# Second attention: the first query weights of each group of heads loaded and split in the key projection's block

## The reference, cut to what matters

```python
q = (x @ Wq).reshape(B, S, 16, 128)      # Wq is 512 x 2048
k = (x @ Wk).reshape(B, S, 4, 128)       # Wk is 512 x 512
v = (x @ Wv).reshape(B, S, 4, 128)
q, k = rope(q), rope(k)
# the two halves of a head's 128 columns are two queries and two keys of 64 columns
a1 = softmax(mask(q1 @ k1.T / 8));  a2 = softmax(mask(q2 @ k2.T / 8))    # window of 128
d = relu(a1 - lam * a2);  d = d / (d.sum(-1) + 1e-6)
x = x + ((d @ v).reshape(B, S, 2048) @ Wo)
```

## Time and profile before

| | us |
|---|---|
| three runs, median (lowest to highest) | 2696.87 (2694.24 to 2699.04) |
| the profiled execution | 2698.5 |
| its span, first to last instruction | 2696.7 |

### The profile page before, as it was taken

One profiled execution on the slowest core, in us unless ns is written; L12 is line 12 of the kernel. 1 busy time (PEld: TensorE's weight loads), 2 busy tenths in 40 slices (PEclk: granted clock), 3 DMA queues, 4 the chain that ended last, 5 costly groups with the idle time before them and its releaser, 6 DMA issues. The chain is left out here.

```text
span 2696.7 us, 35818 instructions
## 1 busy us (share of the span) xinstructions
PE 2519.3 (93%) x12212; PEld 1693.6 (63%) x12212; DVE 1738.9 (64%) x3811; ACT 1112.5 (41%) x2809; POOL 1023.9 (38%) x757
## 2 busy tenths in 40 slices
PE   6899999999599999997879999969999889999998
PEld 3444444443288888886656777657777656557886
DVE  6677676665245555555538999839999823335886
ACT  1246555555232323231316777707776711111111
POOL 2348677775311111110006767615444410002442
PEclk9989999999899999999889999989999999999999
DMA  4721221203300000000212100010000088873101
GB/s 174 242 48 37 43 55 25 56 13 102 125 24 16 16 16 16 16 1 17 92 49 75 44 21 21 21 47 17 17 9 9 1 310 294 292 288 92 48 24 63
DMA packets 153639, 193.64 MB, mean 72 GB/s; under 512 B 52622, under 2 KB 98702, under 8 KB 153088
## 3 DMA queue, kind: packets, MB, share of 16 engines
q1 hardware_dynamic: 141952, 178.90, 20.8%
q0 software_dynamic: 11520, 12.64, 1.5%
HBM read 161.95 MB, written 54.53 MB: 80 GB/s over the span
## 5 line engine op out<-in xcount | busy, mean ns | idle before, releaser
L725 DVE TENSOR_REDUCE neg<-bank 128x1 fp32r<-128x1024 f32 x256 | 300.7, 1213 | 147.0 <-PE bank L629 146.6
L775 ACT ACTIVATE probs<-bank 128x512 f32<-128x512 f32 x512 | 289.4, 596 | 254.0 <-PE bank L639 237.4
L569 POOL TENSOR_TENSOR probs<-probs 128x1024 f32<-128x1024 f32 x128 | 301.9, 2382 | 172.3 <-PE bank L648 172.3
L1567 POOL TENSOR_SCALAR mix<-mix,sm 128x256 f32<-128x256 f32 (+1 forms) x256 | 232.5, 918 | 174.9 <-DVE sm L1464 174.4
L1507 ACT ACTIVATE ms<-ms,sm 128x256 f32<-128x256 f32 (+1 forms) x512 | 247.6, 486 | 94.4 <-DVE sm L1435 93.5
L639 PE MATMUL bank<-q_parts,k_parts 97*128 97x512 f32 x512 | 203.3, 444 | 1.7 <-ACT probs L775 0.7
L947 POOL TENSOR_TENSOR up_lo<-up_raw,up_hi 128x1024 fp32r<-128x1024 f32 x16 | 46.1, 2904 | 401.0 <-ACT up_hi L937 401.0
L1435 DVE CUSTOM_DVE_ANT_0 ms<-bank,misc 128x256 f32<-128x256 f32 (+1 forms) x512 | 184.8, 400 | 2.3
L629 PE MATMUL bank<-k_parts,q_parts 96*128 96x512 f32 x512 | 176.7, 434 | 6.9 <-DVE neg L725 5.0
L639 PEld LDWEIGHTS bank<-q_parts,k_parts 97*128 97x128 f32 x512 | 87.1, 189 | 146.1 <-ACT probs L775 124.2
L1017 DVE TENSOR_TENSOR hid<-bank,sg 128x512 f32<-128x512 f32 x64 | 44.3, 692 | 180.1 <-ACT sg L967 180.1
(11 more groups left out here) (225 smaller groups left out, 5900.9 us busy)
## 6 DMA issues: line engine op xcount, KB each, us to landing
ewg<-in_L_ffn_Wg_dram SPq DMA_DIRECT2D x32, 704.0 KB, 6.8
ewu<-in_L_ffn_Wu_dram SPq DMA_DIRECT2D x32, 704.0 KB, 8.1
ewd<-in_L_ffn_Wd_dram SPq DMA_DIRECT2D x32, 512.0 KB, 5.3
q_parts<-qk_dram SPq DMA_DIRECT2D x48, 256.0 KB, 4.4
up_raw<-in_L_ffn_W_dram SPq DMA_DIRECT2D x16, 512.0 KB, 4.1
ewd<-in_L_ffn_Wd_dram SPq DMA_DIRECT2D x32, 192.0 KB, 5.5
qk_dram<-qk_hi SPq DMA_DIRECT2D x20, 256.0 KB, 2.2
qk_dram<-qk_lo SPq DMA_DIRECT2D x20, 256.0 KB, 2.0
```

The source lines that it names most:

```text
L569: pool.tensor_tensor(probs[:, even, half, :], probs[:, even, half, :], probs[:, odd, half, :], ALU.add).then_inc(S["paired"], 1)
L725: dve.tensor_reduce(neg[:, U % HPT, q:q + 1], bank[:, 2 * (n % 2):2 * (n % 2) + 2, :], AX.XY, ALU.max, negate=True).then_inc(S["max"], 1)
L775: act.activation(probs[:, s % BUFS, j, :], bank[:, 4 + j % 2, :], ACT.Exp, scale=scale).then_inc(S["exps"], 1)
L1567: pool.tensor_scalar(mix[:, p % 2, h, 0:w], mix[:, p % 2, h, 0:w], sm[:, p % 3, 8 + h:9 + h], None, ALU.mult).then_inc(S["probs"], 1)
```

## The change

Pair 0 of each group leaves the heads block. The key block loads its query weights into `w` once VectorE has split the key weights (`klo`), ScalarE and GpSimd split them there into half 0 of `wh` and `wl`, and SyncE loads its output weights after that. The key weights are split into half 1 instead of half 0. In the second group the load of `v` is issued after the query load. In the heads block the four calls for pair 0 are gone; everything else there is as before.

```diff
--- before.py
+++ after.py
@@ -1222,7 +1222,9 @@
 
     ins, xh, xl, bank, ident = (env[k] for k in ("ins", "xh", "xl", "bank", "ident"))
     w, wh, wl, k_, v, rope, lam, tr = (t[k] for k in ("w", "wh", "wl", "k", "v", "rope", "lam", "tr"))
-    rounds = NC * g
+    wo = w[:, :, :].rearrange("p (h a) n -> p h (a n)", h=2)
+    rounds, PAIRS = NC * g, H1 // 4
+    head = 2 * g * PAIRS
 
     @block.sync
     def _(sp):
@@ -1231,9 +1233,20 @@
             sp.dma_start(lam[:, :], ins["L1_attn_lam"].partition_broadcast(P)).then_inc(S["lam"], 16)
             for half in ("woraw", "wraw"):
                 sp.wait_ge(S[half], CREDIT + 16 * NT // 2)
-        else:
+        sp.wait_ge(S["klo"], CREDIT + g + 2)
+        sp.dma_start(w[:, :, :], ins["L1_attn_Wq"].rearrange("(k p) n -> p k n", p=P)[:, :, head * P:(head + 2) * P]).then_inc(
+            S["wraw"], 16)
+        if g:
             sp.dma_start(v[:, :, :], env["v_dram"].rearrange("(n p) d -> p n d", p=P)).then_inc(S["kw"], 16)
+        sp.wait_ge(S["wlo"], CREDIT + g * PAIRS + 1)
+        sp.dma_start(wo, ins["L1_attn_Wo"].rearrange("(h p) n -> p h n", p=P)[:, head:head + 2, :]).then_inc(S["woraw"], 16)
+        if g:
             sp.wait_ge(S["kw"], CREDIT + 64)
+
+    @block.gpsimd
+    def _(pool):
+        pool.wait_ge(S["whi"], CREDIT + g * PAIRS + 1)
+        pool.tensor_tensor(wl[:, 0, :, :], w[:, :, :], wh[:, 0, :, :].bitcast(F32), ALU.subtract).then_inc(S["wlo"], 1)
 
     @block.tensor
     def _(pe):
@@ -1243,7 +1256,7 @@
             for a in range(2):
                 for k in range(KD):
                     for m, (l, r) in enumerate(PARTS):
-                        mm = pe.matmul(bank[:, 2 * (c % 2) + a, :], (wl if l else wh)[:, 0, k, a * P:(a + 1) * P],
+                        mm = pe.matmul(bank[:, 2 * (c % 2) + a, :], (wl if l else wh)[:, 1, k, a * P:(a + 1) * P],
                                        (xl if r else xh)[:, k, c * CH:(c + 1) * CH], start=(k == 0 and m == 0),
                                        stop=(k == KD - 1 and m == 2))
             mm.then_inc(S["proj"], 1)
@@ -1251,7 +1264,7 @@
     @block.vector
     def _(dve):
         dve.wait_ge(S["khi"], CREDIT + g + 2)
-        dve.tensor_tensor(wl[:, 0, :, :], w[:, :, :], wh[:, 0, :, :].bitcast(F32), ALU.subtract).then_inc(S["klo"], 1)
+        dve.tensor_tensor(wl[:, 1, :, :], w[:, :, :], wh[:, 1, :, :].bitcast(F32), ALU.subtract).then_inc(S["klo"], 1)
         if g == 0:
             dve.wait_ge(S["lam"], CREDIT + 32)
             dve.tensor_scalar(lam[:, :], lam[:, :], -1.0, None, ALU.mult).then_inc(S["lam"], 1)
@@ -1266,7 +1279,9 @@
     @block.scalar
     def _(act):
         act.wait_ge(S["kw"], CREDIT + (48 if g else 32))
-        act.activation(wh[:, 0, :, :], w[:, :, :], ACT.Copy).then_inc(S["khi"], 1)
+        act.activation(wh[:, 1, :, :], w[:, :, :], ACT.Copy).then_inc(S["khi"], 1)
+        act.wait_ge(S["wraw"], CREDIT + 16 * (NT // 2 + g * PAIRS + 1))
+        act.activation(wh[:, 0, :, :], w[:, :, :], ACT.Copy).then_inc(S["whi"], 1)
 
 
 def rotate(dve, S, first, second, out1, out2, cos, sin, tr, done, at, names=("cos", "qdone"), halves=(0, 1)):
@@ -1321,8 +1336,6 @@
                 sp.wait_ge(S["wlo"], CREDIT + g * PAIRS + i + 1)
                 sp.dma_start(wo, wo_v[:, head:head + 2, :]).then_inc(S["woraw"], 16)
 
-        query_weights(0)
-        output_weights(0)
         for n in range(NT):
             if g == 0:
                 sp.wait_ge(sent, 16 * TOPK * n)
@@ -1519,7 +1532,6 @@
             act.wait_ge(S["y"], CREDIT + one + NT * i)
             act.activation(woh[:, :, :], wo, ACT.Copy).then_inc(S["wohi"], 1)
 
-        weights_high(0)
         for s in range(UNITS + 3):
             if s < UNITS:
                 exponent(s, 0)
@@ -1572,7 +1584,6 @@
             pool.tensor_tensor(wl[:, i % 2, :, :], raw[:, :, :], wh[:, i % 2, :, :].bitcast(F32),
                                ALU.subtract).then_inc(S["wlo"], 1)
 
-        weights_low(0)
         for c in range(AHEAD):
             rotate(c)
         for s in range(UNITS + 2):
```

## The result

The median of five runs is 2683.28 us (2681.06 to 2685.59), against 2696.87 (2694.24 to 2699.04, five runs) before: 13.6 us less, a ratio of 0.995 with a 95% interval of 0.9937 to 0.9963. The forecast was 2682, with 2676 to 2688 as its range. The profiled execution has a span of 2683.8 us.

What follows compares the result with a forecast made beforehand. TensorE, busy 93% of the span, bounds the kernel, so only its pauses and slow clock offer gain. 2698.5 us less 14.8 gives 2683.7; less 1.6 for the median, 2682.1, say 2682; range 2676 to 2688.

Steps and rivals of the forecast that it cites:

- The chain leaves the heads block: Before each group's first queries, TensorE no longer waits for query-weight load and splits: 7.66 and 7.10 us gained.
- the 14.8 of the sum: Predicted gain of 14.8 us from TensorE's pauses before the first queries of both groups together.
- the block's end: From VectorE's last key rotation to TensorE's first query matmul in the next block: taken as 0.31 us.
- the bounds of 0.26 and 0.88: Lowest and highest cost in us for TensorE crossing the key block's end; 0.88 at both places leaves 13.6 gained.
- The work in the key block is covered: Query load and splits in the key block end by 1377.7 to 1382.4 and 1776.2, before its end: cost nothing.
- SyncE's queue: Second group's v reload, now behind the query load, lands by 1781.1 with 14.6 us of cover: cost nothing.
- The rival that ends slower: Second key block waits for v's reload landing past 1815.9: 2702 us and up, chance 0.04.
- GpSimd beside VectorE: GpSimd's low split may hold a key rotation step at most 2.34 us; counted as nothing; rival 2686.8, chance 0.06.
- the cover that the prediction counted on: VectorE idles 1.66 us before a chunk, three times before the last: 5.0 us, more than the 2.34 held.
- The clock: First query burst of each group stays at half clock, no gain; full-clock rival up to 4.4 us more, chance 0.16.
- the prediction's sign: Wrong if the key block grows, w_lo still ends TensorE's wait, or the shift misses the end of the span.
- two reasons for its 2686: Upper end of the forecast's own range: second twelve query matmuls at half clock, or 0.88 us at each block's end.

Runs made afterwards that it cites:

- the last experiment: The changed kernel with v's reload issued ahead of the wait for the key split, as before the change: 2684.83 us against 2697.98, ratio 0.9951.
- the last two experiments: The changed kernel with GpSimd's low split held until the last key chunk is projected: 2686.63 us; the changed kernel with v's reload issued first: 2684.83 us.

## Why the prediction was right

- *The chain leaves the heads block:* as said. 7.50 + 6.94 = 14.44 us of pause against the 14.8 of the sum. The term that was off is the block's end: TensorE took 0.47 us in both groups, not 0.31, while SyncE and ScalarE took 0.27 and 0.28. It lay within the bounds of 0.26 and 0.88. That the measured 13.6 is also the prediction's sum with 0.88 at both places is chance.
- *The work in the key block is covered:* low splits over 8.1 us (1379.77 - 1371.64) and 7.4 us (1770.28 - 1762.90) after the key split, where 7.8 to 12.5 and 7.2 were worked out; some 20 us to spare.
- *SyncE's queue:* v landed 10.0 us after the key split, where 12.1 was worked out, and its place in the queue did not show in the times or in the pause of the last experiment. The rival that ends slower is out.
- *GpSimd beside VectorE:* in the changed kernel the two did not meet (1379.77 against the first third step at 1380.46, 1770.28 against 1771.73). So the change itself did not test the cover that the prediction counted on; the last two experiments did. Where nothing covers it, the price was 0.92 us a group. Where VectorE has slack it was not quite the nothing of the prediction but 0.65 us, through TensorE, which waited for a bank; the prediction had looked at VectorE's pauses alone. The Trainium skill's rule, SBUF — State Buffer, section SBUF: two separate sides, agrees with the held operations of 1.61 and 2.63 us; by that rule alone, slack left aside, the change would have given back 4.7 us, which it did not.
- *The clock:* counted at half for the first burst of both groups. It was so in the first (4.83 us, as before), in the second it came back early, and the burst took 4.19 us instead of the 4.86 of before (1807.94 - 1803.08):

```profile
1807.94 0.60 PE L1351 MATMUL bank<-xn_hi,w_lo 128*128 128x512 f32 x1
```

 These 0.7 us are luck and not the shorter pause: with the change in the first group alone the second burst took 4.27 us (1802.30 - 1798.03) after a pause of 11.13. Within the bounds, but the reading that led there was weak. I took it from the earlier trace rows that a pause of 3.40 us keeps full clock. The same pause stands before the second key projection in the profiles of the change and of all seven experiments, and in each of the eight the clock was at 0.50 within two us of the restart. In the changed kernel (windows, columns as in the earlier trace rows):

```profile
1764.50:1766.50 2.00, 2.00 (x6) 1.56 (x5) 0.00 (x0) 0.00 (x0) 0.00 (x0) 0.50 0.99 334
```

 The full clock of before was the exception, and it is the +1.54 us of the second key projection in the table. By the prediction's sign the key block should not have grown, and in the second group it did, from 26.64 to 28.18 us; but it took the same 28.18 with the change in the first group alone, where the second key block does only its old work. So the new work in the block is not the cause. With a single profile of before it stays open whether its full clock was chance.
- *The whole:* 13.6 us by the medians against 14.8. Of the 1.2 us between, 0.3 is the block's end. The rest is of the size by which runs of one kernel differ (4 to 5 us from lowest to highest), as the first row of the table is, and no single place in the two profiles accounts for it.
- *The range:* the prediction gives two reasons for its 2686. Only the half clock of a second burst reaches that (2686.5); 0.88 us at each block's end is 13.6 us of gain by its own sum, about 2683.3.

## What to carry to other kernels

At the end of a block look for engines that begin the next one with a load and its preparation one after the other, while the buffers for it were free long before: the pause is the sum of that chain, each link of it can be moved by itself, and what each move takes off the pause is read off the timeline to a few tenths of a us, while the times of whole runs differ by some us. Then look at what ends the pause next; here it was the last rotation of the keys with TensorE's operands at hand, and moving twelve matmuls across the block's end gave another 9.6 us. When work is moved beside another engine, ask where it meets operations that hold it up or are held up by it, whether the last of these has slack, and whether a third engine waits for them meanwhile.

## What the runs showed of the hardware

- TensorE needs longer over a block's end than the others: 0.47 us from VectorE's last instruction to the first matmul, at all ten block ends of six profiles where its data lay ready, against 0.27 for SyncE, 0.28 to 0.36 for ScalarE and 0.39 for VectorE itself.
- The length of a short pause of TensorE did not settle its clock: after 2.91 us one group ran on at 1.00 and the other fell to 0.50, after 3.4 us one profile in nine stayed at 1.00, after 4.45 us the half clock lasted for all twelve matmuls in one group and for some eight in the other, and after 11.13 us for some eight too. What decides it is not shown.
- An operation of VectorE that is held by GpSimd's does not end with it: the two of 0.69 us ended 0.53 and 0.55 us after the split, so most of the operation followed the release. The small one of the earlier trace rows, of 0.16 us, ended 0.02 us after.
